# Second unit of a selective-scan kernel: the softplus of chunk 3 spread over later places

## The reference, cut to what matters

```python
x = silu(dwconv_causal(x, conv_w, conv_b))
x_dbl = x @ xproj_w.T
dt = jax.nn.softplus(x_dbl[..., :R] @ dt_w.T + dt_b)
Bm = x_dbl[..., R:R + N]
Cm = x_dbl[..., R + N:]
...
dA = jnp.exp(dt_t[..., None] * A)
h = h * dA + (dt_t * u_t)[..., None] * B_t[:, None, :]
y = jnp.einsum('bdn,bn->bd', h, C_t)
```

## Time and profile before

| | us |
|---|---|
| median of 3 runs (lowest, highest) | 553.48 (552.98, 554.11) |
| span of the profiled execution | 553.0 |
| busy: DVE, POOL, PE, ACT | 482.0, 474.5, 465.4, 376.9 |
| mean granted TensorE clock | 0.932 of full |

### The profile page before, as it was taken

One profiled execution on the slowest core, in us unless ns is written; L12 is line 12 of the kernel. 1 busy time (PEld: TensorE's weight loads), 2 busy tenths in 40 slices (PEclk: granted clock), 3 DMA queues, 4 the chain that ended last, 5 costly groups with the idle time before them and its releaser, 6 DMA issues.

```text
span 553.0 us, 5691 instructions
## 1 busy us (share of the span) xinstructions
PE 465.4 (84%) x1651; PEld 181.1 (33%) x1651; DVE 482.0 (87%) x591; ACT 376.9 (68%) x666; POOL 474.5 (86%) x157
## 2 busy tenths in 40 slices
PE   2977968869889797979898889888998987795987
PEld 1422413314233242424243433333334332332433
DVE  2675985989898999999989989999999999999951
ACT  1478685687877776776858487868776785364633
POOL 5552799998989989899999998999999999999810
PEclk9999898999989897989799798999898998696999
DMA  4159795959292845838394929294948585830000
GB/s 58 16 51 216 162 204 100 213 142 189 77 216 73 198 112 131 178 93 176 104 189 121 199 87 215 83 199 102 198 120 193 117 178 116 200 74 9 0 11 19
DMA packets 51008, 71.05 MB, mean 128 GB/s; under 512 B 16498, under 2 KB 17442, under 8 KB 50978
## 3 DMA queue, kind: packets, MB, share of 16 engines
q1 hardware_dynamic: 47986, 69.36, 55.4%
q0 software_dynamic: 1024, 1.05, 3.2%
q10 hardware_dynamic: 1968, 0.29, 0.3%
HBM read 60.19 MB, written 10.49 MB: 128 GB/s over the span
## 4 chain that ended last, share of the span: by engine, by line
DVE 37%; PE 35%; issue 15%; ACT 6%; POOL 3%; SPq 2%; DMA 1%; DVEq 0%; ACTq 0%
DVE st L1531 21%; DVE st L1516 9%; PE ps L630 4%; PE ps L729 3%; PE ps L692 3%; PE ps L717 3%; PE ps L811 2%; POOL st L491 2%; PE ps L657 2%; PE ps L700 2%; ACT ps L1096 2%; PE ps L705 2%; PE ps L745 2%; PE ps L669 2%; DVE zr L1537 1%
## 5 line engine op out<-in xcount | busy, mean ns | idle before, releaser
L491 POOL TENSOR_TENSOR st<-st,repC 128x2048 f32<-128x2048 f32 x63 | 285.9, 4541 | 20.3 <-ACT carry L1102 14.9
L1531 DVE TENSOR_TENSOR_SCAN st<-ps,carry,st 128x512 f32<-128x512 f32 x192 | 235.1, 1267 | 4.8 <-ACT ps L1096 3.9
L1096 ACT ACTIVATE ps<-dtS,negA 128x512 f32<-128x512 f32 x256 | 170.9, 681 | 48.7 <-DVE st L1531 47.4
L482 POOL TENSOR_TENSOR st<-duS,repB 128x2048 f32<-128x2048 f32 x30 | 136.3, 4542 | 0.0
L1531 DVE TENSOR_TENSOR_SCAN st<-ps,zero,st 128x512 f32<-128x512 f32 x64 | 78.8, 1269 | 5.8 <-ACT ps L1096 5.5
L717 PE MATMUL ps<-st,fold 128*32 128x512 f32 x504 | 69.6, 625 | 12.8 <-POOL st L491 12.8
L1516 DVE TENSOR_TENSOR st<-duS,ps 128x2048 f32<-128x2048 f32 x33 | 74.9, 2270 | 0.2 <-issue 0.2
L630 PE MATMUL ps<-act,wT 128*128 128x512 f32 x128 | 57.8, 593 | 0.3 <-ACT act L1039 0.3
L463 POOL DMA_INDIRECT x<-in_L_tok_ple_table,idx x32 | 30.5, 953 | 30.8 <-DMA dtS<-dt_dram 14.1
L692 PE MATMUL ps<-xr,Bw 128*128 128x512 f32 x68 | 39.2, 659 | 7.9 <-ACT bc_sb L1088 5.4
L669 PE MATMUL ps<-xr,wT 128*32 128x512 f32 x32 | 20.6, 731 | 22.2 <-DVE st L1516 22.2
(11 more groups left out here) (141 smaller groups left out, 635.9 us busy)
## 6 DMA issues: line engine op xcount, KB each, us to landing
repC<-bc_dram SPq DMA_DIRECT2D x64, 256.0 KB, 10.5
duS<-du_dram SPq DMA_DIRECT2D x60, 256.0 KB, 4.5
dtS<-dt_dram SPq DMA_DIRECT2D x60, 256.0 KB, 7.5
repB<-bc_dram SPq DMA_DIRECT2D x60, 128.0 KB
dt_dram<-dt SPq DMA_DIRECT2D x16, 256.0 KB, 3.1
du_dram<-du SPq DMA_DIRECT2D x16, 256.0 KB, 2.0
bc_dram<-bc_sb SPq DMA_DIRECT2D x16, 64.0 KB
dtS<-dt_dram SPq DMA_DIRECT2D x8, 128.0 KB, 3.3
```

The source lines that it names most:

```text
L482: pool.tensor_tensor(st[:, r], duS[:, u % 2], row, ALU.mult).then_inc(sem("dbu_pool"), 1)
L491: pool.tensor_tensor(st[:, r], st[:, r], row, ALU.mult).then_inc(sem("hc_ready"), 1)
L1096: sc.activation(decay_bank(u, r, q), dtS[:, u % 2, q], ACT.Exp, scale=negA[:, way(u), q, r:r + 1]).then_inc(sem("decay_ready"), 1)
L1531: dve.tensor_tensor_scan(st[:, r, q, order], decay_bank(u, r, q)[:, order], st[:, r, q, order], first, ALU.mult, ALU.add).then_inc(sem("sc ...
```

## The change

In unit 1 alone, the softplus of chunk 3 is taken apart. On ScalarE `dt_out(2)` goes from place 0 to place 2, ahead of `bc_out(3)`; `softplus_in(3)` goes to place 3, `softplus_exp(3)` to place 4, `softplus_plus1(3)` and `softplus_ln(3)` to place 5, and `dt_out(3)` from place 8 to place 10, ahead of `new_x(0)`. On VectorE `log1p_error(3)` goes from place 0 to place 6. On TensorE `sum_dt(3)` goes from behind `bc(3)` to behind `partial(0)`. No instruction is added or removed, and the lists of POOL and SP are the same.

```diff
@@ TensorE, the list of unit u
                 if u + 2 < UNITS:
                     bc(u + 2)
-                if u + 2 < UNITS:
+                if 3 < u + 2 < UNITS:
                     sum_dt(u + 2)
                 if is_unit(u - 1):
                     sum_states(u - 1, 3)
...
                 if u - 2 in QUICK:
                     hidden(u - 2, 0)
+                if u == 1:
+                    sum_dt(u + 2)
                 if is_unit(u):
                     add_nought(1)
                     sum_states(u, 0)
@@ ScalarE, between(u, p)
                     if u != 1 and u + 2 < UNITS:
                         softplus_exp(u + 2)
+                    if u != 1 and u + 2 < UNITS:
+                        softplus_plus1(u + 2)
+                    if u != 1 and u + 2 < UNITS:
+                        softplus_ln(u + 2)
+                if p == 2:
                     if u == 1:
                         dt_out(2)
-                        softplus_in(u + 2)
-                        softplus_exp(u + 2)
-                    if u + 2 < UNITS:
-                        softplus_plus1(u + 2)
-                    if u + 2 < UNITS:
-                        softplus_ln(u + 2)
-                if p == 2:
                     if u + 2 < UNITS:
                         bc_out(u + 2)
+                if u == 1 and p == 3:
+                    softplus_in(3)
+                if u == 1 and p == 4:
+                    softplus_exp(3)
+                if u == 1 and p == 5:
+                    softplus_plus1(3)
+                    softplus_ln(3)
+                if u == 1 and p == 10:
+                    dt_out(3)
...
                 if p == 8:
-                    if u + 2 < UNITS:
+                    if u != 1 and u + 2 < UNITS:
                         dt_out(u + 2)
@@ VectorE, between(u, p)
-                    if u + 2 < UNITS:
+                    if u != 1 and u + 2 < UNITS:
                         log1p_error(u + 2)
...
+                if u == 1 and p == 6:
+                    log1p_error(3)
```

## The result

| | before | changed |
|---|---|---|
| median (lowest, highest), us | 553.23 (551.73, 554.11), 4 runs | 558.88 (557.94, 560.47), 4 runs |
| ratio, 95% interval | | 1.009 (1.0054 to 1.0126) |
| span of the traced execution, us | 553.0 | 556.2 |
| mean granted clock | 0.932 | 0.926 |

The medians differ by 5.65 us; the ratio makes it 5.0, between 3.0 and 7.0 by the interval. The forecast was 556.0 with a range up to 557.7: the sign is right, the size is not. The ratios and intervals here leave out runs of more than 1.5% above the fastest of the same kernel, the medians and means take in all. The traced execution of the changed kernel took 557.99 us in all, 1.8 us more than its span, and the runs since show 1.8 to 1.9. By the same difference the traced execution of before took about 554.8 us (an estimate, no time of it is known), not the 553.0 that I had set equal to its span.

The account below looks back on a forecast made before the run. No engine bounds the kernel alone; from 99.39 to 116.83 the end hangs on the PE list. 1.45 us for PE order plus 1.05 for low clock, 2.5 on the median 553.48, gave 556.0, range 554.0 to 557.7.

Parts of the forecast that it names:

- Part 3: PE before way_out(0): a 3.8 us hole lowers the clock for the work behind it, costing 1.05 us more.
- the sum: Whole kernel: 1.45 + 1.05 = 2.5 us on the median of 553.48 gives 556.0, unit 1's delay passed on in full.
- Part 1: DVE at the head of unit 1: waits of 4.1 and 0.5 us replace 5.82; y_by_z(0) starts at 97.0.
- Part 2: PE list in unit 1: sum_dt(3) waits for the later correction, so conv(4) and the burst come 1.45 us later.
- Rival D: DVE's lead comes through if sum_dt(3) can start before 99.9: up to 1.4 us faster, 552.1; chance 0.07.
- the upper bound: PE from way_out(0) at 97.7: clock low from there on, 6.0 us of work, 2.3 us more.
- rival B: PE clock low from way_out on, DVE's by_gate waiting as well: 1.45 + 2.3 us, 557.2; chance 0.20.
- the middle case: PE behind the hole: low clock from about 98.95 costs 1.05 us, the forecast of 556.0; chance 0.43.
- the 102 to 103: PE in unit 1: sum_dt(3) starting at 102 to 103 us would show the forecast right.
- The sum, base: Whole kernel: the span of 553.0 taken as also the lowest timed run; the 2.5 us added to the median 553.48.
- I pass the delay to the end in full: Behind unit 1: the chain is tight, without gaps, so the 2.5 us reaches the end with nothing added.

Follow-up runs that it names:

- e4: The changed kernel with bc_out(3) on ScalarE moved from place 2 to place 4, behind two more decays; median 553.67 us, ratio 0.9994 to before.
- e9: The changed kernel with three products with zeros on PE between bc(3) and the last fold of unit 0; median 554.09 us, ratio 1.0027 to before.
- e6: The kernel before with four more products with zeros on PE in unit 1, between partial result and fold; median 556.38 us, ratio 1.0061.
- e1: The changed kernel again, unaltered, beside the kernel before; median 558.37 us, ratio 1.0101.
- e5: The kernel before again, unaltered, for a second trace and more timed runs; median 553.82 us, ratio 0.9995.
- e11: The kernel of e8 once more, to see whether its gain stands; median 551.41 us, ratio 0.9931 to before.
- e2: The changed kernel with four products with zeros on PE between bc(3) and the last fold of unit 0; median 557.83 us, ratio 1.0072 to before.
- e3: The kernel before with only sum_dt(3) moved behind partial(0) on PE, ScalarE and VectorE as before; median 559.96 us, ratio 1.0111.
- e8: The kernel of e4 with chunk 3's exp, +1, Ln and bc_out at place 4, correction behind y_by_z, sum_dt(3) behind the skip product; median 551.87 us, ratio 0.9961.
- e13: The changed kernel with two more products with zeros (1.72 us) at add_nought in unit 1 on PE; median 561.17 us, ratio 1.0109 to before.
- e12: The changed kernel with one more product with zeros (0.86 us) at add_nought in unit 1 on PE; median 558.01 us, ratio 1.0079 to before.

## Why the prediction was wrong in size

Two terms failed: the 1.05 us for the low clock (Part 3), and the nothing that I added for what lies behind unit 1 (the sum). In traces the first measured 1.0 to 2.3 us, 1.8 on average; the second shows in the timed means as 1.5 us (plus or minus 1.1) beyond what P explains. With the first alone put right the forecast would have been some 556.7, still within its range.

**Part 1 (DVE's hole mostly kept): right.** Expected were 4.1 and 0.5 us of waiting and `y_by_z` at 97.0; measured 4.06, 0.57 and 96.89. e4 shows the cause: with `bc_out(3)` out of the way the wait for `decay(1, 0, 3)` is 0.24 us, and `y_by_z(0)` comes as soon as the fold is done.

**Part 2 (the PE list, 1.45 us): right.** e9, with the clock full, has 1.47, and there `sum_dt(3)` starts 9.70 behind `bc(3)`, the forecast having 9.64. My own steps give 101.41 + 2.77 - 102.67 = 1.51, not 1.45, which changes nothing. Rival D, that the burst does not hang on the list, falls with e6. The condition that I named for D, `decay(1, 0, 3)` free of `bc_out(3)`, was built in e4: the loss went, and unit 1 became 1.0 us shorter than before.

**Part 3 (the clock, 1.05 us): mechanism right, the term mis-sized.** I took over the pattern of the nearest row, a low clock that begins 1.3 us after the work is back. In all four traces it was low before `way_out` began. In e1 it came back 3.1 us after `way_out` began, and the term was 1.0, about the size that I had taken; in the other three it lasted into the partial result, and the term was 2.0 to 2.3, near the upper bound and rival B, `by_gate`'s wait included. So the 1.0 of e1 agrees by luck: low clock lay over another part of the work than I had assumed. The average of the four is 1.8. I had given rival B 0.20 and the middle case 0.43. My arithmetic was off as well: 2.03 us in the ratio of 1.87 to 1.02 is 3.72, not 3.6, and the term by its own steps is then about 1.3, the forecast 556.2. `sum_dt(3)` came at 103.31, just outside the 102 to 103 that I had named as a sign. The Trainium skill (TensorE: Matmul & The Clock Gate, Loop structure matters more than you think) has matmuls run cold behind a long wait, its example being a wait for a DMA; all four traces agree (3.41 to 4.14 us of hole, products at 0.50). The Trainium skill (TensorE: Matmul & The Clock Gate, Part 1) advises to leave the ramp out of a model as under 1% of a span. As a share that agrees with this term (1.8 us is 0.3% of the span), but it would have missed more than half of the loss on this stretch: 1.45 in place of 3.3.

**The sum, base: misread, without effect.** "the span of 553.0, which is also the lowest of the timed runs" treated the span as the time. With 1.8 us around the span the traced run took about 554.8, above the median: an execution with one of the dearer patterns of the clock (407.8 us for units 2 to 15, against 405.1 in e5). The forecast was added to the median, so its number does not rest on this.

**The sum, "I pass the delay to the end in full": incomplete.** In the first pair of traces it holds, and e6 shows that a delay alone costs about its length. But the timed means differ by 4.8 (plus or minus 0.9), and P by 3.3. The missing 1.5 us goes with low clock: 11 us more a run than before, of which unit 1 explains about 6 (6.8 us in three traces, 3.4 in e1). All four traces of the changed kernel have dear patterns behind unit 1 (407.8, 410.8, 407.9 and 408.1 us), while e4, e5, e9 and e11 took 404.2 to 405.2 (the first trace of before took 407.8, and e2, e3, e6 and e8 lie between 406.8 and 410.2). Over all sixteen traces, the eight with the clock low around `way_out` took 408.4 on average, the eight without 406.5: 1.9 us less, plus or minus 1.7. In three of the four, unit 2 starts at nearly the same distance (18.2, 18.1, 17.9 us) behind the return of the clock. That the low clock of unit 1 sets this distance, and with it the pattern, was my theory L, and it isn't the whole of it: the first trace of before and e6, with no low clock there, took the same 407.8 and 407.9. What makes the stretch behind unit 1 dearer, and why e13 is dear again, stays open.

## What to carry to other kernels

When a stall is closed by spreading a chain over later places, look at what an instruction that waits for another engine has queued behind it, and at which list the end really hangs on in that stretch: here DVE won 1.8 us and PE, which counted, lost 3.3. Here holes of 3.4 to 4.1 us on TensorE cost 1.0 to 2.3 us more through the clock on the work behind them, and filling them with idle products kept the clock up in both versions, though only the one with three products showed it in the time. Where runs of one kernel differ by 1% with the granted clock, a single trace fits only its own pattern: add the time around the span, and compare means of many runs.

## What the runs showed of the hardware

- The same program met the clock differently from run to run: low from 96.1 to 102.9 in the first trace and from 96.7 to 100.2 in e1, which makes 1 us of difference in P.
- The time of the kernel before varies from 549.5 to 559.4 us, with a mean granted clock of 0.956 to 0.923 (the shorter runs have the higher one), while P stays at 10.91 in both traces.
- 2.6 us of added work on PE ahead of the fold (e9) lowered the mean by 4.1 us, plus or minus 1.6, from 558.5 to 554.4; 3.4 us of it there (e2) left it at 557.9, and 0.86 us behind the partial result (e12) at 557.7, both within the scatter of the changed kernel's.
